# A two-layer graph kernel on one core: the next graph's features prepared one round ahead, all five queues reordered

## What is computed

```python
def _gat(h, adj, W, a, out_features):           # layer 0, twice
    Wh = jnp.matmul(h, W)
    e = leaky_relu(Wh @ a[:F] + (Wh @ a[F:]).swapaxes(1, 2), 0.2)
    att = jax.nn.softmax(jnp.where(adj > 0, e, NEG), axis=1)
    return jnp.matmul(att, Wh)
# layer 0: x1 = LN(x + gat(gat(x)));  x2 = LN(x1 + relu(x1 @ w_ff1) @ w_ff2)
# layer 1: eight heads; attention probabilities are masked by adj == r and each
#          mask has its own values v_r = x2 @ Wv[r]; then @ Wo
#          x3 = LN(x2 + attn); out = LN(x3 + gelu(x3 @ W1) @ W2)
```

## Time and profile before

| | |
|---|---|
| median of 3 runs | 3356.56 us (3351.75 to 3358.59) |
| the profiled execution's own time | 3361.25 us |
| its span, first to last instruction | 3359.4 us |
| mean granted PE clock | 0.986 of full |
| PE / PE weight loads busy | 94% / 85% |
| DVE / ACT / POOL busy | 71% / 66% / 53% |
| chain that ended last | PE 86%, DVE 9%, issue 3%, ACT 1% |
| moved by DMA | 93.43 MB, 28 GB/s |

### The profile page before, as it was taken

One profiled execution on the slowest core, in us unless ns is written; L12 is line 12 of the kernel. 1 busy time (PEld: TensorE's weight loads), 2 busy tenths in 40 slices (PEclk: granted clock), 3 DMA queues, 4 the chain that ended last, 5 costly groups with the idle time before them and its releaser, 6 DMA issues.

```text
span 3359.4 us, 79402 instructions
## 1 busy us (share of the span) xinstructions
PE 3151.1 (94%) x27864; PEld 2840.8 (85%) x27864; DVE 2376.6 (71%) x5298; ACT 2228.8 (66%) x5770; POOL 1772.1 (53%) x1481
## 2 busy tenths in 40 slices
PE   4799999999999999999999999999999999999996
PEld 3688888888888888888888888888888888888885
DVE  4577776776776776776776776776776776776763
ACT  2466676676677677677677677677677676676673
POOL 1355555555555555555555555555555555555554
PEclk7899999999999999999999999999999999999998
DMA  5000000000000000000000000000000000000000
GB/s 127 20 27 29 22 28 28 22 28 28 22 28 28 23 27 28 25 25 28 26 25 28 27 24 27 28 25 25 28 25 25 28 25 25 28 25 25 28 10 14
DMA packets 98850, 93.43 MB, mean 28 GB/s; under 512 B 9856, under 2 KB 98048, under 8 KB 98816
## 3 DMA queue, kind: packets, MB, share of 16 engines
q1 hardware_dynamic: 98816, 92.97, 9.2%
HBM read 76.17 MB, written 16.78 MB: 28 GB/s over the span
## 4 chain that ended last, share of the span: by engine, by line
PE 86%; DVE 9%; issue 3%; ACT 1%; SPq 1%; POOL 0%; DMA 0%; DVEq 0%; POOLq 0%; ACTq 0%
PE ps_f L246 11%; PE ps_f L247 10%; PE ps_f L248 10%; PE ps_ao L436 7%; PE ps L426 7%; PE ps L246 4%; PE ps L248 4%; PE ps L247 4%; PE ps L416 4%; DVE s_least L819 4%; PE ps_ao L246 3%; PE ps_ao L247 3%; PE ps_ao L248 3%; PE ps_g L246 3%; PE ps_g L248 3%
## 5 line engine op out<-in xcount | busy, mean ns | idle before, releaser
L964 POOL TENSOR_TENSOR hid_lo<-hid_full,hid_hi 128x512 fp32r<-128x512 f32 x512 | 722.3, 1416 | 853.8 <-ACT hid_hi L601 847.0
L246 PE MATMUL ps_f<-down_w_hi,hid_hi 128*128 128x256 f32 x2048 | 602.1, 294 | 1.6 <-ACT hid_full L597 0.8
L247 PE MATMUL ps_f<-down_w_lo,hid_hi 128*128 128x256 f32 x2048 | 571.1, 279 | 0.0
L248 PE MATMUL ps_f<-down_w_hi,hid_lo 128*128 128x256 f32 x2048 | 570.7, 279 | 0.0
L616 ACT ACTIVATE prob<-ps,s_least 128x256 f32<-128x256 f32 x1024 | 471.3, 483 | 58.4 <-DVE s_least L819 57.5
L947 POOL TENSOR_TENSOR rstd<-vareps,neg_half 128x2 f32<-128x2 f32 x256 | 205.0, 801 | 442.0 <-DVE vareps L766 442.0
L246 PEld LDWEIGHTS ps_f<-down_w_hi,hid_hi 128*128 128x128 f32 x2048 | 384.4, 188 | 51.4 <-issue 45.3
L771 DVE TENSOR_SCALAR norm<-norm,meanvar,rstd 128x256 f32<-128x256 f32 x512 | 251.4, 533 | 198.4 <-POOL rstd L947 192.9
L247 PEld LDWEIGHTS ps_f<-down_w_lo,hid_hi 128*128 128x128 f32 x2048 | 386.9, 189 | 0.0
L828 DVE SCALAR_TENSOR_TENSOR masked<-adj_in,prob 128x1024 f32<-128x1024 int32 x256 | 386.9, 1550 | 0.0
L248 PEld LDWEIGHTS ps_f<-down_w_hi,hid_lo 128*128 128x128 f32 x2048 | 386.4, 189 | 0.0
(11 more groups left out here) (158 smaller groups left out, 9754.5 us busy)
## 6 DMA issues: line engine op xcount, KB each, us to landing
adj_in<-adj_keys SPq DMA_DIRECT2D x128, 256.0 KB, 2.8
xT_in<-x_features SPq DMA_DIRECT2D x64, 256.0 KB, 2.7
norm<-x_nodes SPq DMA_DIRECT2D x64, 256.0 KB, 2.7
out_nodes<-norm SPq DMA_DIRECT2D x64, 256.0 KB, 2.2
raw_up<-L_w_ff SPq DMA_DIRECT2D x1, 1024.0 KB, 5.5
raw_down<-L_w_ff SPq DMA_DIRECT2D x1, 1024.0 KB, 8.4
raw_v<-L_Wv SPq DMA_DIRECT2D x4, 256.0 KB, 7.6
raw_up<-L_W SPq DMA_DIRECT2D x1, 1024.0 KB, 9.2
```

Source lines behind the costliest of these rows:

```text
L246: nc.tensor.matmul(ps_out, left[0], right[0], start=first, stop=False)
L247: nc.tensor.matmul(ps_out, left[0], right[1], start=False, stop=False)
L248: return nc.tensor.matmul(ps_out, left[1], right[0], start=False, stop=last)
L964: pool.tensor_tensor(hid[1][:, 2 * m:2 * m + 2, :], hid_full[:, 2 * m:2 * m + 2, :], value(hid[0][:, 2 * m:2 * m + 2, :]), ALU.subtract).t ...
```

## The change

A fifth role, `nxt` with graph e = t+3, is added to each body. `pe_gat_rows`, `pe_gat_cols` and `pe_gat_wh1` for l = 0, `dve_fence`, `dve_gat_in` and `pool_gat_in` are called for e near the end of round t instead of for c at the head of the next one. The round's boundary moves with them: `pe_scores(a, 0)`, `pe_wo(b)`, `pe_prob_turn(a, 0, ·)` and `pe_up(c, 0, 1)` now stand at the end of a round. `pe_qk` is called ahead of the last attention product, `pe_scores(a, 0)` behind it and the last three `pe_down` behind that. `run` gets one more partial round ahead (-3), and round B-3 leaves the loop to stand behind it without its `nxt` steps; `sp_run` and every function that issues instructions stay as they are, so each graph has the same instructions as before. Lists of ACT, DVE and POOL are reordered to suit.

```diff
--- before.py
+++ after.py
@@ -480,28 +480,15 @@
                                     start=(k == 0), stop=(k == C - 1))
     last.then_inc(wo_done.sem, 1)
-def pe_body(pe, t, gat, ff0, att1, ff1):
-    a, b, c, d = t + 1, t, t + 2, t - 1
-    if att1:
-        pe_scores(pe, b, 0)
-    if ff1:
-        pe_wo(pe, d)
-    if gat:
-        pe_gat_rows(pe, c, 0)
-        pe_gat_cols(pe, c, 0)
-        pe_gat_wh1(pe, c, 0)
-    if ff0:
-        pe_up(pe, a, 0, 1)
-    if att1:
-        pe_prob_turn(pe, b, 0, 0)
-        pe_prob_turn(pe, b, 0, 1)
+def pe_body(pe, t, nxt, gat, ff0, att1, ff1):
+    a, b, c, d, e = t + 1, t, t + 2, t - 1, t + 3
     if ff0:
         pe_up(pe, a, 0, 2)
+    if att1:
+        pe_scores(pe, b, 1)
+    if ff0:
         pe_up(pe, a, 0, 3)
-    if att1:
-        pe_scores(pe, b, 1)
-    if ff0:
         pe_down(pe, a, 0, 0, 0)
     if gat:
         pe_gat_mix(pe, c, 0)
@@ -510,14 +497,14 @@
     if ff0:
         pe_down(pe, a, 0, 0, 1)
         pe_down(pe, a, 0, 1, 0)
+        pe_down(pe, a, 0, 1, 1)
     if att1:
         pe_reach(pe, b)
-    if ff0:
-        pe_down(pe, a, 0, 1, 1)
+    if gat:
+        pe_gat_rows(pe, c, 1)
     if att1:
         pe_v(pe, b, 0)
     if gat:
-        pe_gat_rows(pe, c, 1)
         pe_gat_cols(pe, c, 1)
         if isinstance(t, int) and t == -2:
             pe_setup(pe)
@@ -535,34 +522,48 @@
         pe_prob_turn(pe, b, 1, 1)
     if ff1:
         pe_up(pe, d, 1, 0)
-        pe_up(pe, d, 1, 1)
     if att1:
...
     if ff1:
+        pe_up(pe, d, 1, 1)
         pe_up(pe, d, 1, 2)
...
         pe_up(pe, d, 1, 3)
+        pe_down(pe, d, 1, 0, 0)
+    if ff0:
+        pe_qk(pe, a)
     if att1:
         pe_av_all(pe, b, 1)
         pe_av_one(pe, b, 1)
-    if ff1:
-        pe_down(pe, d, 1, 0, 0)
+    if gat:
+        pe_turn(pe, c, 0)
+    if att1:
+        pe_av_more(pe, b, 1)
+    if ff0:
+        pe_scores(pe, a, 0)
+    if ff1:
         pe_down(pe, d, 1, 0, 1)
         pe_down(pe, d, 1, 1, 0)
-    if att1:
-        pe_av_more(pe, b, 1)
-    if gat:
-        pe_turn(pe, c, 0)
-    if ff1:
         pe_down(pe, d, 1, 1, 1)
-    if ff0:
-        pe_qk(pe, a)
+    if att1:
+        pe_wo(pe, b)
     if gat:
         pe_up(pe, c, 0, 0)
+    if nxt:
+        pe_gat_rows(pe, e, 0)
+        pe_gat_cols(pe, e, 0)
+    if ff0:
+        pe_prob_turn(pe, a, 0, 0)
+    if nxt:
+        pe_gat_wh1(pe, e, 0)
+    if ff0:
+        pe_prob_turn(pe, a, 0, 1)
+    if gat:
+        pe_up(pe, c, 0, 1)
 def act_gat_pre(act, g, l):
@@ -630,22 +631,24 @@
     act.activation(rec_rows[:, hg, :], ps_ao[:, 0, (1 - hg) * N:(2 - hg) * N],
                    ACT.Copy).then_inc(rec_rows_set.sem, 1)
-def act_body(act, t, gat, ff0, att1, ff1):
-    a, b, c, d = t + 1, t, t + 2, t - 1
+def act_body(act, t, nxt, gat, ff0, att1, ff1):
+    a, b, c, d, e = t + 1, t, t + 2, t - 1, t + 3
     if att1:
         act_prob(act, b, 0, 1)
-    if gat:
+    if ff0:
+        act_hidden(act, a, 0, 0)
+    if att1:
+        act_prob_turned(act, b, 0, 0)
+    if gat:
+        act_gat_pre(act, c, 0)
         act_gat_wh(act, c, 0)
-        act_gat_pre(act, c, 0)
+    if att1:
+        act_prob_turned(act, b, 0, 1)
     if ff0:
         act_hidden(act, a, 0, 1)
-    if att1:
-        act_prob_turned(act, b, 0, 0)
     if gat:
         act_gat_exp(act, c, 0)
-    if att1:
-        act_prob_turned(act, b, 0, 1)
     if ff0:
         act_hidden(act, a, 0, 2)
         act_hidden(act, a, 0, 3)
@@ -664,10 +667,9 @@
         act_prob_turned(act, b, 1, 0)
     if gat:
         act_gat_wh(act, c, 1)
+        act_gat_exp(act, c, 1)
     if ff0:
         act_turned(act, a, 1)
-    if gat:
-        act_gat_exp(act, c, 1)
     if ff1:
         act_hidden(act, d, 1, 0)
     if att1:
@@ -677,14 +679,12 @@
         act_hidden(act, d, 1, 1)
         act_hidden(act, d, 1, 2)
         act_hidden(act, d, 1, 3)
+    if ff0:
+        act_qk(act, a)
+    if gat:
+        act_turned(act, c, 0)
     if att1:
         act_ao(act, b, 1)
-    if gat:
-        act_turned(act, c, 0)
-    if ff0:
-        act_qk(act, a)
-    if gat:
-        act_hidden(act, c, 0, 0)
     if ff0:
         act_prob(act, a, 0, 0)
@@ -863,49 +863,44 @@
     dve.tensor_tensor(ao[:, hg, :], ps_ao[:, 0, hg * N:(hg + 1) * N], rec_rows[:, hg, :],
                       ALU.mult).then_inc(ao_set.sem, 1)
-def dve_body(dve, t, gat, ff0, att1, ff1):
-    a, b, c, d = t + 1, t, t + 2, t - 1
-    if gat:
-        dve_fence(dve, c)
-        dve_gat_in(dve, c)
-    if att1:
-        dve_least(dve, b, 0, 0)
-        dve_least(dve, b, 0, 1)
+def dve_body(dve, t, nxt, gat, ff0, att1, ff1):
+    a, b, c, d, e = t + 1, t, t + 2, t - 1, t + 3
+    if gat:
+        dve_gat_wh12(dve, c, 0)
     if ff1:
         dve_norm(dve, d, 2)
     if att1:
-        dve_adj_top(dve, b)
-    if gat:
-        dve_gat_wh12(dve, c, 0)
-    if ff1:
-        dve_norm_end(dve, d, 2)
+        dve_rec(dve, b, 0, 0)
+        dve_rec(dve, b, 0, 1)
     if gat:
         dve_gat_score(dve, c, 0)
         dve_gat_wh(dve, c, 0)
+    if ff1:
+        dve_norm_end(dve, d, 2)
+    if gat:
         dve_gat_split(dve, c, 0)
...
         dve_mask(dve, b, 0)
-        dve_rec(dve, b, 0, 0)
-        dve_rec(dve, b, 0, 1)
     if ff1:
         dve_turned(dve, d, 2)
-    if att1:
-        dve_least(dve, b, 1, 1)
-        dve_reach(dve, b)
-        dve_rec(dve, b, 1, 0)
     if gat:
...
             dve_setup(dve)
+    if att1:
+        dve_rec(dve, b, 1, 0)
+        dve_least(dve, b, 1, 1)
+        dve_reach(dve, b)
     if ff0:
...
         dve_rec(dve, b, 1, 1)
+    if gat:
+        dve_gat_wh12(dve, c, 1)
+    if att1:
         dve_v(dve, b, 0)
-    if gat:
-        dve_gat_wh12(dve, c, 1)
     if ff0:
         dve_norm_end(dve, a, 1)
     if gat:
@@ -914,27 +909,35 @@
         dve_v(dve, b, 1)
         dve_flag(dve, b)
         dve_v_more(dve, b)
+        dve_mask_more(dve, b, 0)
     if gat:
         dve_gat_wh(dve, c, 1)
-    if att1:
-        dve_mask_more(dve, b, 0)
+        dve_gat_split(dve, c, 1)
     if ff0:
         dve_turned(dve, a, 1)
-    if gat:
-        dve_gat_split(dve, c, 1)
     if att1:
         dve_ao(dve, b, 0)
         dve_mask(dve, b, 1)
-        dve_mask_more(dve, b, 1)
     if gat:
         dve_norm(dve, c, 0)
         dve_norm_end(dve, c, 0)
+    if nxt:
+        dve_fence(dve, e)
+    if att1:
+        dve_mask_more(dve, b, 1)
+    if gat:
         dve_turned(dve, c, 0)
+    if att1:
+        dve_ao(dve, b, 1)
+    if ff0:
+        dve_least(dve, a, 0, 0)
+    if nxt:
+        dve_gat_in(dve, e)
+    if ff0:
+        dve_least(dve, a, 0, 1)
+        dve_adj_top(dve, a)
     if ff1:
         dve_norm(dve, d, 3)
-    if att1:
-        dve_ao(dve, b, 1)
-    if ff1:
         dve_norm_end(dve, d, 3)
@@ -974,40 +977,41 @@
     pool.tensor_copy(rec_wide[:, hg, :, :].rearrange("p c (h d) -> p c h d", d=DH),
                      cols[:, hg, :, :].unsqueeze(3).broadcast_to([P, C, HG, DH])).then_inc(rec_wide_set.sem, 1)
-def pool_body(pool, t, gat, ff0, att1, ff1):
-    a, b, c, d = t + 1, t, t + 2, t - 1
-    if gat:
-        pool_gat_in(pool, c)
-        if isinstance(t, int) and t == -2:
-            pool_setup(pool)
-    if ff0:
-        pool_hidden(pool, a, 0, 0)
-    if ff1:
-        pool_rstd(pool, d, 2)
-    if ff0:
-        pool_hidden(pool, a, 0, 1)
-        pool_hidden(pool, a, 0, 2)
-        pool_hidden(pool, a, 0, 3)
-    if att1:
-        pool_rec_wide(pool, b, 0)
-        pool_affine(pool, b, 1)
-    if ff0:
-        pool_rstd(pool, a, 1)
+def pool_body(pool, t, nxt, gat, ff0, att1, ff1):
+    a, b, c, d, e = t + 1, t, t + 2, t - 1, t + 3
     if att1:
         pool_rec_wide(pool, b, 1)
     if ff1:
-        pool_affine(pool, d, 2)
         pool_hidden(pool, d, 1, 0)
         pool_hidden(pool, d, 1, 1)
         pool_hidden(pool, d, 1, 2)
-        pool_hidden(pool, d, 1, 3)
     if gat:
...
     if ff1:
+        pool_hidden(pool, d, 1, 3)
+    if nxt:
+        pool_gat_in(pool, e)
+    if ff1:
         pool_rstd(pool, d, 3)
         pool_affine(pool, d, 3)
+    if gat:
+        pool_hidden(pool, c, 0, 0)
+    if ff0:
+        pool_rec_wide(pool, a, 0)
+    if att1:
+        pool_rstd(pool, b, 2)
+    if gat:
+        pool_hidden(pool, c, 0, 1)
+        pool_hidden(pool, c, 0, 2)
+        pool_hidden(pool, c, 0, 3)
+    if att1:
+        pool_affine(pool, b, 2)
+    if ff0:
+        pool_affine(pool, a, 1)
+    if gat:
+        pool_rstd(pool, c, 1)
 def rows(w):
@@ -1203,19 +1207,23 @@
     eng.wait_ge(prep_p.sem, PREP_P)
-def run(eng, body):
+def run(eng, body, setup=None):
     gat_ready(eng)
-    body(eng, -2, True, False, False, False)
+    body(eng, -3, True, False, False, False, False)
+    if setup:
+        setup(eng)
+    body(eng, -2, True, True, False, False, False)
     ready(eng)
-    body(eng, -1, True, True, False, False)
-    body(eng, 0, True, True, True, False)
-    body(eng, 1, True, True, True, True)
-    with eng.Fori(2, B - 2) as t:
```

(52 more changed lines are left out.)

4 lines of the change are left out of this document (removed).

## The result

| | before | after |
|---|---|---|
| median | 3355.08 us (3351.75 to 3358.59, 4 runs) | 3397.49 us (3394.83 to 3400.45, 4 runs) |
| profiled execution / its span | 3361.25 / 3359.4 us | 3400.45 / 3398.7 us |
| mean granted PE clock | 0.986 | 0.972 |

The ratio is 1.0126, with a 95% interval of 1.0109 to 1.0144: **slower by 42 us**, where 3241 us and a gain were forecast. The forecast gave that side a chance of 0.03.

The account below looks back on a forecast made before the run. PE, 94% busy, was taken as the bound: its list plus two gaps a round. From 3361.3 us, -123 + 12 + 0 - 5 = -116 gave 3245, and 3241 us as median; range 3212 to 3290 us.

Parts of the forecast that it names:

- (a) The gaps: PE's waits before the first graph product and the attention row's turn: both closed, 2.02 us a round, -123 us.
- (b) Thin margins: Five PE steps with 0.1 to 0.5 us of room, the mix among them: 0.2 us a round, +12 us.
- The bound of +73 us: Upper bound for the steps with little room: 1.2 us a round, one long mask plus 0.2 at another step.
- PE's own steps wider than 0.118: Sign of being wrong: PE's split matmuls of 256 columns following each other at more than 0.118 us.
- The rule weighed: DVE and POOL exclude each other on a shared port; one more such meeting before a thin step: about 1 us a round.
- (c) Entries: PE going from fp32 or a turn into split products: five real fp32 stretches before and after, 0 us.
- (d) DMA: Adjacency transfers on SP's unchanged list: in time or covered, nothing added.
- (e) The ends: First 260 us and round 62, outside the steady rounds: -5 us, bounds -12 and +3.
- Rival 2: DVE's chain into the flag or ACT's into ps_f comes 1 us late each round: 3290 us, chance 0.18.
- Rival 4: Slower: late pool_rstd(b, 2) holds dve_norm_end and DVE's split before the mix; 3387 us at 4.0 late, chance 0.03.
- the waits announced as late next: PE's expected remaining waits, for more_flag, v_sb, hid_full and att_s_lo: together under 15 us.

Follow-up runs that it names:

- experiment 3: The changed kernel with twelve useless split matmuls on PE in its wait ahead of the first layer's mix: 3336.36 us, ratio 0.9933.
- experiment 2: The changed kernel with POOL waiting for the end of DVE's split before its last two hidden steps: 3279.52 us, ratio 0.9763.
- experiment 5: experiment 2 with a pe_down moved between the last attention product and the scores, making one fp32 stretch into two: 3294.83 us, ratio 0.9821.
- Experiment 6: The changed kernel with POOL held until the split ends and DVE's split moved ahead of dve_norm_end(d, 2): 3263.53 us, ratio 0.9728.
- attempts 7 to 9: Experiment 6 with pool_affine(d, 2) a round later, 3269.32 us; with both affine steps behind the masks, 3279.96 us; the latter with reach before row minimum, 3278.35 us.

## Why the prediction was wrong, point by point

**(a) The gaps: right.** Both waits of the earlier trace rows are gone. PE's list takes 50.06 - 2.00 = 48.06 us, where 48.3 was worked out; of the 0.25 less, 0.1 is that a wait is followed by one matmul at 0.22 instead of 0.118 and there is one wait in place of two, and the rest isn't accounted for. The mix was due at 1606.51, 5.5 us into the round, as in the prediction's list (whose 0, the start of up 2, is 1601.03 in the timeline).

**(b) Thin margins: the step that failed.** The sentence is "The mix waits for DVE's split, 1.73 us (...) after the exponentials end at 3.1, 5.0 against 5.5", priced with its neighbours at 0.2 us a round and at 1.2 at the most. Measured, the split begins at 1604.70, which is 3.7, and ends at 1608.4, which is 7.4. Of the 2.4 us, 2.0 are the pair at `L733` (2.90 for 0.88). The rest stands ahead of it in DVE's list, where the scalings take 1.44 for 0.74 and `L766` 1.17 for 0.17; no run parts these two. The durations were right as those of a kernel in which POOL idled at that moment; they were carried over to a list in which it no longer does. The margin to look at was not the 0.5 us in front of PE but another: before, POOL's next subtraction started 1596.25 - 1595.57 = 0.68 us behind the end of the pair. In the kernel before, the scalings stood ahead of the scores, and DVE had 1.20 us of idle time in front of the split; the change calls them between the two, a POOL operation beside them adds 0.7, nothing is left to absorb it, and the pair moves into POOL's next work. The bound of +73 us was also built from one long mask in place of a median one, and not from the row of the split: an instruction that shows no spread in the trace (475 to 487 ns) was taken as one that has none.

**The clock: a term that was missing.** "PE's own steps wider than 0.118" stood among the signs of being wrong, and it came, but the sum had no term for it: it was put at nothing, without a reason. It cost 61 us (experiment 3), more than the whole loss of 42. The forecast added idle times as if PE started again at full speed behind each. Behind the two idle times of the earlier trace rows, 1.31 and 0.47 us, the granted clock is 1.00; nothing there said what one of 2 us would do, and the forecast didn't bound it.

**The rule weighed.** The prediction cited the Trainium skill, "SBUF — State Buffer", section "SBUF: two separate sides", for DVE and POOL locking each other out, and the runs agree: `L733` goes from 0.48 to 1.56 us where an operation of POOL's runs beside it, and back to 0.48 in experiment 2. It was priced there at "about 1 us a round" in front of a thin step, which is a right price for one meeting. There were four ahead of the mix (`L766` with 1.17 us, the scalings, and each of the pair). The lists of both engines were at hand: POOL's `pool_hidden(c, 0, 2)` and `(c, 0, 3)` came at 4.4 and 5.9 us, the time of the split.

**(c) Entries: right.** Five stretches of fp32 before and after, so 0; experiment 5 adds one and pays 0.26 us a round. **(d) DMA: right**, no wait names one. **(e) The ends:** -9.4 by the account, with the first rounds, for -5.

**The rivals.** Rival 2, a new wait in place of the old, was the right kind, but put at 1 us and at the flag or `ps_f`. Rival 4, the slower one, had the right place (a late split in front of the mix, behind `dve_norm_end`) and the wrong cause: `rstd` is done at 1602.68, 1.65 us into the round, against 1.5 in the prediction, so POOL's list was read rightly and nothing came late from there. Its 3387 us lies near the result by luck, since it has neither the stretched pair nor the clock. Of the waits announced as late next, the kernel after shows only the one for `att_s_lo`; those for the flag, `v_sb` and `hid_full` had their margins widened by the wait ahead of them. Experiment 6, where that wait is gone, shows the flag late by 0.2 us and the rows of the second layer, which the prediction didn't list, by 0.4.

**What stays open.** Why the clock falls in 40 rounds and holds in 17 with the same wait isn't settled. Two or three long rounds are followed by a short one in the steady part, and the fall doesn't begin at a fixed distance behind the wait: at 1557.7 it is 0.9 us behind PE's restart, in the next round, at 1608.9, it is 0.4 us, and in the round after that it doesn't come. Nor was it tested whether the length of a gap or its place in the round decides. That a version without contention in the first half of the round would reach the 48.3 us, some 3230 us in all, wasn't shown: the attempts 7 to 9 moved it only.
